# Narrower memsets between the first pass's scatters of sorted rows

## The chip, the cores and the metric

The kernel runs on one core of a Trainium2 chip. The metric is the device time of one execution in microseconds, smaller is better. Before the change it is 570.33 us, the median of three runs (570.11 to 571.1).

## The reference, cut to what matters

A block on 2 x 1024 tokens of 128 features: a mixture-of-experts layer, attention, and the same mixture again, each on a layer norm of its input.

```python
x = x + 0.5 * ffn(layernorm(x), ...)
x = x + attn(layernorm(x), ...)
x = x + 0.5 * ffn(layernorm(x), ...)

def ffn(x, sg, su, sd, rg, ru, rd, wr, rb):
    shared_out = expert(x, sg, su, sd)                  # silu(x g^T) * (x u^T), times d
    probs = softmax(x @ wr.T + rb)                      # 7 routed experts
    scores, idx = top_k(probs, 2)
    w = weights of the two, summing to 1
    out = shared_out
    for e in range(7):
        out = out + w[..., e:e + 1] * expert(x, rg[e], ru[e], rd[e])
    return out
```

## The kernel before, in words

Each token goes through the shared expert and through two of seven routed experts. Instead of computing every expert for every token, the kernel sorts: each normalised row (130 floats: 128 features, the token's number and a code for its rank) is written to DRAM (`z_rows`) at a place that belongs to its expert, twice, once for each of its two experts. Rows are then read back in tiles of 128 that belong to one expert. The first mixture layer is called the first pass here (f = 0), the one after attention the second (f = 1).

**The work of a pass.** TensorE goes through 54 jobs in a fixed order (`JOBS`): in the first pass 13 tiles of the shared expert, 38 routed tiles, and the last 3 shared tiles. A job is an up-projection (`up_pe`, L899 to L901), a multiplication with the silu on ScalarE (L1000) and VectorE (`act_dve`, L1043), three transposes (`act_tr_pe`, L919), a down-projection (`down_pe`, L933) and a copy or an addition out of PSUM (`yev_dve`, L1079 and L1081). A step of the loop in `ffn_pe` handles the up-projection of one job, the transposes of the one before and the down-projection of the one before that. Routed tiles come in batches (`BATCHES`: tiles 0-1, 2-5, 6-9, 10-11, 12-13, then fours). A batch's rows are transposed by `rows_tr_pe` (L953) when its loads have landed.

**The order of the sort.** The tokens are handled in two halves of 8 tiles. For each half VectorE computes a router (`router_dve`), the place of every row (`places_dve`, which ends with the cast to `slots`, L750), and then the lists of tiles (`segments_dve`, `lists_dve`, which ends with `rows_at`: L863 in the first half, L865 in the second). In the first 47 us VectorE also splits the routed weights in two parts: four operations of L1482, with both operands in SBUF.

GpSimd (POOL in the profile) runs `sort_part_pool` for the first and then the second half: 16 scatters each, in the order of the tiles, two for each tile. A scatter (`sort_pool`, L1174) is one indirect DMA of 128 rows. It waits for nothing of its own; the half as a whole waits for its `slots`. Behind each scatter whose tile is not the first one comes `pause_pool`: a memset (L1184) of 128 x 384 bf16 in a scratch tile, `idle`, which waits until the previous such memset is done. So the first two scatters of a pass have no memset behind them, and the other 30 have one. Nothing reads `idle`.

Behind the sort on POOL's queue come the scatters of results (`scatters_pool`, L1197), one for each routed tile, the first ten of them with the same memset, the next ones in the first pass with a memset of `keys` (L1415).

SyncE (SP) loads the sorted rows (`rows_load_sp`): it reads the tiles' places into registers (L1253), waits until all 16 scatters of the half have landed (`z_sc`), and issues one load for each tile (L1260, 65 KB). Batches 0 to 2 (tiles 0 to 9) need the first half only. Batch 3, whose first tile is tile 10, and all later ones need the second half, its lists, and 7 small DMAs of zeros that SyncE issues between the two (`pads_sp`, L1241).

The results ring has 8 buffers (`RING_Y`): VectorE's copy of routed tile n waits until the scatter of tile n - 8 has landed.

The memset in question, and what calls it:

Of the kernel before, what the change touches and what calls it, by code (L numbers as in the profile page):

```python
# [22 lines left out]
F32 = mybir.dt.float32  # L23
# [6 lines left out]
P = 128  # L30
# [33 lines left out]
HALF = TT // 2  # L64
# [219 lines left out]
def place_memory(K, ctx):  # L284
# [4 lines left out]
    def sb(name, shape, dt=F32, scope=ctx):  # L289
        return scope.enter_context(K.nc.sbuf_tensor(name, shape, dt))  # L290
# [59 lines left out]
    with ExitStack() as s:  # L350
        zt = [sb(f"zt_{part}", [P, TOKENS], F32R, scope=s) for part in ("h", "l")]
        with ExitStack() as s2:
# [8 lines left out]
            K.ys = sb("ys", [P, RING_Y, EMB], scope=s2)  # L361
            K.idle = sb("idle", [P, PAUSE], BF16, scope=s2)
            K.col_i = sb("col_i", [P, 2 * NJ + TT], mybir.dt.int32, scope=s2)
# [802 lines left out]


PAUSE = 3 * P


def sort_pool(K, f, g):

    e, (r, t) = K.nc.gpsimd, divmod(g, TT)
    e.indirect_dma_start(K.z_dram[f], bass.IndirectOffsetOnAxis(ap=K.slots[:, g:g + 1], axis=0),  # L1174
                         K.zrow[f][:, t, :], None).then_inc(K.z_sc[t // HALF], 16)
    if g % TT > 0:
        pause_pool(K, f == 1 and t < HALF)


def pause_pool(K, in_attention=False):  # L1180

    rested_pool(K)
    where = K.queries[2][:, 0:PAUSE].bitcast(F32) if in_attention else K.idle[:, :]
    K.nc.gpsimd.memset(where, 0.0).then_inc(K.rested, 1)  # L1184
    K.rests += 1


def rested_pool(K):

    if K.rests:  # L1190
        K.nc.gpsimd.wait_ge(K.rested, K.rests)
# [9 lines left out]
def sort_part_pool(K, f, h, first=0, last=SPAN):  # L1201

    e, (t0, t1) = K.nc.gpsimd, PARTS[h]
    if first == 0:
        if f == 1:
            e.wait_ge(K.blank_rows[f], 16 * FILLS * LOOPED)
        e.wait_ge(K.numbered, 2 * f + h + 1)
        e.wait_ge(K.NS[2 * f]["z"], t1 // TPC)
        e.wait_ge(K.RS["slot"], routed(f, h, "slot", 5))
    for g in [r * TT + t for t in range(t0, t1) for r in range(2)][first:last]:  # L1210
        sort_pool(K, f, g)


def scatters_pool(K, f):

    for j in range(NJ):
        if j == BATCHES[BATCH_OF[j]][0]:
            K.nc.gpsimd.wait_ge(K.FF[f]["ids"], 3 * BATCH_OF[j] + 3)
        scatter_pool(K, f, j)
        if j < WHOLE:  # L1220
            pause_pool(K)
        elif f == 0 and j < WHOLE + 2 * WIPES:
            wipe_pool(K, *divmod(j - WHOLE, WIPES))
        if f == 0 and j in FRONT_POOL:
            norm_rstd_pool(K, 1, FRONT_POOL[j])
# [1133 lines left out]
```

## Time and profile before

| | |
|---|---|
| median of 3 runs | 570.33 us |
| profiled execution | 571.84 us |
| its span, first to last instruction | 570.0 us |
| mean granted clock of TensorE | 0.972 of full |
| TensorE matmul busy | 521.1 us (91%) |
| VectorE busy | 388.5 us (68%) |
| ScalarE busy | 319.8 us (56%) |
| POOL busy | 272.1 us (48%) |

Times in the profile are microseconds from the start of the span. PE is TensorE, PEld its weight loads, DVE VectorE, ACT ScalarE, POOL GpSimd, SP SyncE. L1174 is line 1174 of the kernel. In a timeline a row has its start, its length, engine, line, operation, what it writes and reads, and in brackets how long the engine stood idle before it and what released it. The record of a scatter on POOL is the time that POOL spends on it; the data land later.

### The profile page before, as it was taken

What the parts mean: (1) busy time and instruction counts of PE and PEld (TensorE: products, weight loads), DVE (VectorE), ACT (ScalarE), POOL (GpSimd) and SP (SyncE); (2) the same over time, 40 slices, a digit from 0 to 9 for tenths busy, and PEclk for the clock granted to TensorE, in tenths of its full rate; (3) what the DMA queues carried; (4) which work ended last, traced back from release to release, by engine and by line L of the source; (5) the groups of instructions that cost most, each with busy time, mean ns of one, the idle gap of its engine ahead of it and who ended that gap; (6) DMA issues with size and microseconds to landing.
All of it is one profiled execution on the core that took longest, in us unless ns stands there. A gap on an engine that the chain in (4) does not pass through costs nothing.

```text
span 570.0 us, 11374 instructions
## 1 busy us (share of the span) xinstructions
PE 521.1 (91%) x3574; PEld 406.0 (71%) x3574; DVE 388.5 (68%) x1013; ACT 319.8 (56%) x678; POOL 272.1 (48%) x417
## 2 busy tenths in 40 slices
PE   5985969999996799999999999999999889889995
PEld 2884969998954465656666666565746889889995
DVE  5694635557367888887979888888555775445744
ACT  4552424457444276776767677677776444434643
POOL 8299887667356711212120303030318888854540
PEclk9899789999996899999999999999999999999999
DMA  8922424132861581505050505020001031431414
GB/s 283 294 67 50 111 77 120 45 107 81 242 183 56 170 190 35 173 2 175 2 174 1 176 0 176 1 102 2 2 2 33 31 91 43 118 92 34 125 50 121
DMA packets 41384, 54.65 MB, mean 96 GB/s; under 512 B 6064, under 2 KB 32176, under 8 KB 40560
## 3 DMA queue, kind: packets, MB, share of 16 engines
q1 hardware_dynamic: 32528, 42.70, 26.4%
q0 software_dynamic: 4480, 9.25, 4.9%
q10 hardware_dynamic: 4320, 1.98, 1.3%
q8 instruction: 32, 0.52, 0.4%
q14 instruction: 24, 0.20, 0.1%
HBM read 34.03 MB, written 28.00 MB: 109 GB/s over the span
## 4 chain that ended last, share of the span: by engine, by line
PE 57%; issue 18%; POOL 10%; DMA 6%; DVE 4%; SPq 2%; ACT 2%; ACTq 1%; another core or an unknown queue 1%; POOLq 0%; DVEq 0%
PE psum L1605 11%; PE psum L1648 11%; PE psum L1677 10%; PE psum L933 6%; POOL z_rows L1174 6%; PE psum L919 3%; PE psum L901 3%; PE psum L899 3%; PE psum L900 3%; PE psum L1608 2%; POOL idle L1184 2%; DMA b_p<-in_attn_c_proj_b 2%; DMA yc<-y_rows 1%; DMA y_rows<-ys,to_row 1%; PE psum L1633 1%
## 5 line engine op out<-in xcount | busy, mean ns | idle before, releaser
L1757 DVE TENSOR_REDUCE mxp<-psum 128x1 f32<-128x512 f32 (+3 forms) x304 | 179.0, 654 | 32.9 <-PE psum L1605 32.1
L1816 ACT ACTIVATE probs<-psum 128x512 f32<-128x512 f32 (+1 forms) x304 | 154.9, 578 | 39.8 <-PE psum L1648 37.2
L1863 POOL TENSOR_SCALAR_AFFINE_SELECT probs<-probs 128x512 f32<-128x512 f32 x64 | 40.0, 635 | 174.2 <-ACT probs L1816 174.2
L1648 PE MATMUL psum<-queries,keys 128*128 128x512 f32 (+3 forms) x384 | 122.5, 381 | 0.6 <-DMA queries<-m_rows 0.3
L1605 PE MATMUL psum<-keys,queries 128*128 128x512 f32 (+1 forms) x304 | 116.1, 417 | 2.9 <-DVE mxp L1757 2.4
L1000 ACT ACTIVATE silu<-psum 128x352 f32<-128x352 f32 x107 | 49.6, 463 | 99.5 <-PE psum L901 62.6
L1197 POOL DMA_INDIRECT y_rows<-ys,to_row x76 | 74.3, 977 | 59.1 <-DVE ys L1079 35.4
L1043 DVE TENSOR_TENSOR act<-silu,psum 128x352 f32<-128x352 f32 x107 | 55.6, 519 | 68.0 <-ACT silu L1000 41.7
L933 PE MATMUL psum<-wall_f,at 128*128 (+1 forms) x648 | 92.2, 279 | 2.7 <-DVE x L1081 1.8
L1648 PEld LDWEIGHTS psum<-queries,keys 128*128 128x128 f32 x384 | 66.8, 191 | 26.8 <-ACT probs L1816 12.6
L933 PEld LDWEIGHTS psum<-wall_f,at 128*128 128x128 f32 x648 | 82.1, 194 | 4.1 <-ACT at L1008 2.3
L1605 PEld LDWEIGHTS psum<-keys,queries 128*128 128x128 f32 x304 | 58.1, 194 | 18.1 <-DVE mxp L1757 7.8
L1677 PE MATMUL psum<-probs,vg 128*32 128x512 f32 (+3 forms) x768 | 69.8, 491 | 0.4 <-POOL probs L1863 0.4
L919 PE MATMUL psum<-ident,act 128*128 128x128 f32 x324 | 54.7, 278 | 5.9 <-DVE act L1043 4.4
L899 PE MATMUL psum<-wall,zs_h 128*128 x152 | 56.9, 374 | 1.0 <-issue 1.0
L1008 ACT COPY at<-psum 128x384 f32<-128x384 f32 x108 | 51.3, 475 | 11.0 <-PE psum L919 9.7
L900 PE MATMUL psum<-wall,zs_h 128*128 x152 | 50.4, 331 | 0.0
L901 PE MATMUL psum<-wall,zs_l 128*128 x152 | 50.2, 330 | 0.0
L919 PEld LDWEIGHTS psum<-ident,act 128*128 128x128 f32 x324 | 41.0, 142 | 12.3 <-DVE act L1043 8.2
L1677 PEld LDWEIGHTS psum<-probs,vg 128*32 128x32 f32 x768 | 21.1, 109 | 35.4 <-issue 22.9
L1174 POOL DMA_INDIRECT z_rows<-zrow,slots x32 | 34.4, 1076 | 15.9 <-DVE slots L750 10.5
L1174 POOL DMA_INDIRECT z_rows<-zrow_late,slots x32 | 31.2, 975 | 5.8 <-issue 5.8
(240 smaller groups left out, 732.4 us busy)
## 6 DMA issues: line engine op xcount, KB each, us to landing
z_rows<-q_stack SPq DMA_DIRECT2D x12, 682.5 KB, 5.6
keys<-k_stack SPq DMA_DIRECT2D x32, 128.0 KB, 5.9
queries<-q_stack SPq DMA_DIRECT2D x8, 512.0 KB, 5.3
zg_early<-z_rows SPq DMA_DIRECT2D x44, 65.0 KB
yc<-y_rows SPq DMA_DIRECT2D x10, 256.0 KB, 4.0
zg_late<-z_rows SPq DMA_DIRECT2D x32, 65.0 KB
k_stack<-zt_h SPq DMA_DIRECT2D x8, 256.0 KB, 2.9
q_stack<-q_h SPq DMA_DIRECT2D x8, 256.0 KB, 3.7
```

Source lines behind the costliest of these rows:

```text
L899: e.matmul(dst, zh, weight(K.wall, base, hi, HID), start=True, stop=False)
L900: e.matmul(dst, zh, weight(K.wall, base, lo, HID), start=False, stop=False)
L901: ins = e.matmul(dst, zl, weight(K.wall, base, hi, HID), start=False, stop=True)
L919: ins = e.transpose(bank(K, at_bank(f, q))[:, k * P:(k + 1) * P], K.act[:, q % 2, k * P:(k + 1) * P], K.ident[:, :])
L933: ins = e.matmul(bank(K, Y_BANK)[:, 0:EMB], K.at[:, q % 2, k * P:(k + 1) * P], weight(K.wall_f, base, DN + k * EMB, EMB), start=(k == 0), ...
L1174: e.indirect_dma_start(K.z_dram[f], bass.IndirectOffsetOnAxis(ap=K.slots[:, g:g + 1], axis=0), K.zrow[f][:, t, :], None).then_inc(K.z_sc[t ...
L1197: e.indirect_dma_start(K.y_dram[f], bass.IndirectOffsetOnAxis(ap=K.to_row[:, j:j + 1], axis=0), K.ys[:, j % RING_Y, :], None).then_inc(K.y ...
L1605: ins = e.matmul(dst, K.queries[u][:, i * P:(i + 1) * P], K.keys[u][:, heads[0]:heads[-1] + 1, k0 * P:(k0 + nb) * P], start=True, stop=Tru ...
L1648: ins = e.matmul(slot(K, u, d, n)[:, m * (q1 - q0):(m + 1) * (q1 - q0)], K.keys[v][:, j, kt * P:(kt + 1) * P], K.queries[v][:, q0:q1], sta ...
L1677: ins = e.matmul(bank(K, O_BANK)[32 * j:32 * j + 32, q0 - half * CHUNK:q1 - half * CHUNK], K.vg[:, kt, j, :], probs_of(K, n)[:, j, :], sta ...
L1757: e.tensor_reduce(K.mxp[:, heads[0]:heads[-1] + 1, i, which], scores, AX.X, ALU.max).then_inc(K.A["taken"], 1)
L1816: e.activation(probs_of(K, product)[:, heads[0]:heads[-1] + 1, :], src, ACT.Exp, scale=SCALE).then_inc(K.A["ex"], 1)
```

## The change

A memset behind a scatter of the first pass (f = 0) writes 32 columns of `idle` instead of 384. Those of the second pass, and those behind the first ten scatters of results in either pass, keep 384. The number of memsets, their order and their waits stay.

```diff
 PAUSE = 3 * P
+SHORT = P // 4
...
     if g % TT > 0:
-        pause_pool(K, f == 1 and t < HALF)
+        pause_pool(K, f == 1 and t < HALF, PAUSE if f else SHORT)


-def pause_pool(K, in_attention=False):
+def pause_pool(K, in_attention=False, columns=PAUSE):

     rested_pool(K)
-    where = K.queries[2][:, 0:PAUSE].bitcast(F32) if in_attention else K.idle[:, :]
+    where = K.queries[2][:, 0:PAUSE].bitcast(F32) if in_attention else K.idle[:, 0:columns]
     K.nc.gpsimd.memset(where, 0.0).then_inc(K.rested, 1)
```

## Rows read from the trace of the kernel before

**Rows 1.** Timeline of TensorE, the first tile behind each of two stalls

```profile
56.44 0.50 PE L953 MATMUL psum<-ident,zg_early 128*128 128x128 f32 x2 [4.90 <-DMA zg_early<-z_rows]
...
82.05 0.66 PE L953 MATMUL psum<-ident,zg_early 128*128 128x128 f32 x2 [4.67 <-DMA zg_early<-z_rows]
```

**Rows 2.** The page: busy tenths of TensorE in 40 slices of 14.25 us

```profile
PE   5985969999996799999999999999999889889995
```

**Rows 3.** The chain of waits, 76 to 82.2 us: start, length, what

```profile
76.18 2.39 DMA z_rows<-zrow,slots
...
79.76 1.88 DMA zg_early<-z_rows
```

**Rows 4.** The scatters of the first pass: duration min/median/max, first and last start

```profile
L1174 POOL DMA_INDIRECT z_rows<-zrow,slots x32: 958/964/2375, 24.8 to 76.2; - x32
```

**Rows 5.** Timeline of POOL, 24 to 53 us

```profile
26.31 0.96 POOL L1174 DMA_INDIRECT z_rows<-zrow,slots  x1 [0.30 <-issue]
27.57 0.96 POOL L1174 DMA_INDIRECT z_rows<-zrow,slots  x1 [0.30 <-issue]
...
29.13 1.52 POOL L1174 DMA_INDIRECT z_rows<-zrow,slots  x1 [0.17 <-issue]
...
32.81 0.96 POOL L1174 DMA_INDIRECT z_rows<-zrow,slots  x1 [0.16 <-issue]
...
43.48 2.38 POOL L1174 DMA_INDIRECT z_rows<-zrow,slots  x1 [0.16 <-issue]
...
51.13 0.96 POOL L1174 DMA_INDIRECT z_rows<-zrow,slots  x1 [0.17 <-issue]
52.70 0.96 POOL L1174 DMA_INDIRECT z_rows<-zrow,slots  x1 [0.16 <-issue]
```

**Rows 6.** Groups of POOL's instructions by shape: count, busy us, mean ns, idle before

```profile
L1184 POOL MEMSET idle<- 128x384 bf16 x66 | 28.7, 434 | 0.0
...
L1374 POOL MEMSET d_used<- 128x9 f32 x1 | 0.1, 97 | 0.0
```

**Rows 7.** Timeline of VectorE, 28 to 73 us

```profile
28.56 1.25 DVE L1482 TENSOR_TENSOR wall<-nat_g,wall 128x1056 fp32r<-128x1056 f32 x1
...
33.49 1.61 DVE L1482 TENSOR_TENSOR wall<-nat_g,wall 128x1408 fp32r<-128x1408 f32 x1
...
37.67 1.25 DVE L1482 TENSOR_TENSOR wall<-nat_u,wall 128x1056 fp32r<-128x1056 f32 x1
...
43.40 1.61 DVE L1482 TENSOR_TENSOR wall<-nat_u,wall 128x1408 fp32r<-128x1408 f32 x1
...
46.85 0.54 DVE L750 CAST slots<-d_slot 128x16 int32<-128x16 f32 x1
...
72.77 0.25 DVE L865 SCALAR_TENSOR_TENSOR rows_at<-d_raw,d_start,tile 128x28 int32<-128x28 f32 x1
```

**Rows 8.** Register loads of the tiles' places on SyncE: min/median/max ns

```profile
L1253 SPq TENSOR_LOAD <-rows_at x22: 463/872/1068, 35.7 to 503.8; - x22
```

**Rows 9.** Stretches: length, busy time by engine, granted clock, DMA share, GB/s

```profile
77.00:80.50 3.50, 0.39 (x4) 0.19 (x2) 0.71 (x2) 0.37 (x2) 3.17 (x6) 1.00 0.19 57
80.50:82.00 1.50, 0.00 (x0) 0.00 (x0) 0.00 (x0) 0.00 (x0) 1.33 (x3) 0.51 0.43 107
486.44:488.31 1.87, 0.00 (x1) 0.03 (x1) 0.33 (x2) 0.00 (x0) 1.55 (x3) 1.00 0.49 141
```

**Rows 10.** Timeline of TensorE: up-projections behind the second stall

```profile
82.37 0.64 PE L899 MATMUL psum<-wall,zs_h 128*128 x1
...
88.82 0.41 PE L899 MATMUL psum<-wall,zs_h 128*128 x1
...
93.19 0.41 PE L899 MATMUL psum<-wall,zs_h 128*128 x1
```

**Rows 11.** DMA queues, 24 to 29 us: packets, MB, share of 16 engines

```profile
q0 software_dynamic: 4, 0.01, 1.3%
```

## The prediction

> **What bounds the kernel now.** I read the waits of TensorE first, then its timeline around the longest ones, then the chain of waits back from there, and last the timelines of the engines that the chain names. Between 40 and 90 us TensorE stands still twice for gathered rows [rows 1]. The first gathered tile is transposed at 56.44 after 4.90 us without work, so the shared tiles ahead of it end at 51.54; the eleventh tile, the first of the second half's list, comes at 82.05 after 4.67, so TensorE was free at 77.38. From 85.5 to 171 us every slice of the page has TensorE busy nine tenths or more [rows 2], so what the second stall gives up moves everything behind it.
>
> The chain behind the second stall [rows 3]: the last scatter starts at 76.18 and lands 2.39 later, SyncE issues the loads, the load takes 1.88, and TensorE starts at 82.05. That is 5.87 us from the start of the 32nd scatter. The first stall has the same form: the 16th scatter starts at 51.13 [rows 5], and TensorE follows 5.31 us later. POOL works through the 32 scatters in one piece, from 24.8 to 76.2 with a median of 964 ns each [rows 4], and is on the chain all that time.
>
> **What a pause costs.** Two scatters with no memset between them start 1.26 us apart (26.31, 27.57); with one, 1.57 (51.13, 52.70) [rows 5]: 0.96 for the scatter, 0.43 for the memset, 0.17 until the next. A memset of 384 columns takes 434 ns and one of 9 columns 97 [rows 6], 0.90 ns a column, so I put one of 32 columns at 0.12 (estimate from the two). Then 0.96 + 0.12 + 0.17 = 1.25, no less than the 1.26 that scatters take without a memset, and I take 1.26. Each pause gives 0.305. The lower end is nothing at all, if a scatter grows by what the pause loses (a rival below); the upper is 0.315.
>
> **First half.** 13 pauses stand ahead of the 16th scatter; 13 x 0.305 would be 4.0. But scatters are also held up by VectorE. L1482 runs four times with two operands in SBUF [rows 7], and a scatter that starts inside one is long: that of 29.13 ends at 30.65, 0.84 after the op's end at 29.81; that of 43.48 (2.38 long) ends at 45.86, 0.85 after 45.01 [rows 5, 7]; the two others repeat the pattern. As an undisturbed scatter lasts 0.96, it seems to need what VectorE holds (the port, below) some 0.12 after its start. With that I walk the new order, VectorE's times left as they are. The 4th starts at 28.83 inside the first op and ends at 30.65 as before. The 7th starts at 33.47, needs the port at 33.59, inside the op of 33.49, and ends at 35.94 as before. The 9th starts at 37.50, needs it at 37.62, just before the op of 37.67, and goes through; the 10th (38.76) ends at 39.76. The 14th starts at 43.84 inside the last op and ends at 45.85, so the 15th starts at 46.15 and the 16th at **47.41 instead of 51.13: 3.7 us**. If the 9th is caught after all (0.05 decides), the 16th starts at 48.67: 2.5. If the 7th escapes too, 5.0. I take 3.7.
>
> The second half's scatters wait for their places (the cast L750, done at 47.39 [rows 7]). The 17th would start at 48.67, so it does not wait. Of POOL's queue nothing else stands between.
>
> **Second half.** 16 steps from the 16th to the 32nd, 0.305 each: 4.9 us. Two lists ops of VectorE in that stretch also have two operands in SBUF and could hold a scatter for up to 0.5 each; they are short beside a step of 1.26, so I take off 0.2 (ends 0 and 1.0). The last scatter then starts at 76.18 - 3.7 - 4.9 + 0.2 = 67.8 and its rows reach TensorE at 67.8 + 5.87 = 73.7: **8.4 us** earlier.
>
> **Is TensorE there by then, and what is late next?** It starts the routed tiles at 47.41 + 5.31 = 52.7 and had 20.8 us of work from there to the second stall; part of that ran at half clock after the first stall, which now is 1.2 us. Without it TensorE is ready at about 71.1 and waits 2.6 us. The places of the second half's tiles (L865) are ready at 73.02 today [rows 7], 16.6 after the first gathered tile. They follow TensorE's steps, so they come at 52.7 + 16.6 - 2.4 = 66.9; with SyncE's register load, 0.87 [rows 8], 67.8. The landing of the last scatter, 67.8 + 2.39 = 70.2, is still the later one. The scatters of results that are queued behind on POOL start 8.4 us earlier as well and keep their own 384-column pauses; their first is needed when its ring slot comes round, eight tiles later, so they cost nothing.
>
> **The clock of TensorE.** After the 4.67 us stall the granted clock was 1.00 until 80.5, 3.1 us after the last matmul, then 0.51; a stall of 1.87 us in the second pass kept 1.00 [rows 9]. At 1.2 GHz, from the first up-projection at 82.37 to the third at 88.82, the work took 6.45 us; the next two tiles at 2.4 GHz, with a larger batch to transpose, took 4.37 (88.82 to 93.19) [rows 10]. Allowing 0.3 for the first transposes and the smaller batch, the low clock costs 2.4. The new second stall of 2.6 lies between the two cases. Gain: 2.4 if the clock stays, 0 if it falls as before, -0.7 if it falls just as TensorE resumes (1.5 us more of work at the low clock, at 2.4 per 5.25). The nearer row is the one that falls, so I take 1.0.
>
> **Sum:** 3.7 + 4.9 - 0.2 + 1.0 = 9.4 us. Against the profiled execution's 571.84 (span 570.0 and 1.84 around it, which the change does not touch) that gives 562.4; the runs shown have a median of 570.33, 1.5 less, so the forecast is 561.0 us.
>
> **Rivals.**
> *The lists become the bound* (0.14). Denser scatters hold up VectorE's small casts: L750 took 0.54 for 16 columns [rows 7]. Five such ops stand in the lists of the second half; if each waits one scatter more (0.96), they end 4.8 later, 2.4 past the last landing's margin of 2.4 (70.2 - 67.8). The gain falls to 7.0, or 6.0 if the clock falls: 563 to 564.5. Against: VectorE came in between POOL's ops so far.
>
> *The op that starts first holds the port* (0.07). Then the 9th scatter, started 0.17 before L1482, would delay that op to 38.46; it would end at 39.71, the 10th scatter at 40.55 instead of 39.76, and the gain is 0.8 less: 561.8. The trace speaks against it: a scatter started at 32.81 [rows 5] and L1482 still began inside it at 33.49 and took its usual 1.61 [rows 7]. The Trainium skill (SBUF — State Buffer, SBUF: two separate sides) has this rule: whichever of the two starts first has the shared pair for the whole instruction and the other blocks fully. By that rule the time is 561.8; the trace agrees that a scatter inside L1482 is blocked, not that L1482 is blocked by a scatter.
>
> *The queue of scatters fills: slower* (0.08). POOL starts scatters faster than they land. If only two may be on their way, a step is at least half a landing: 1.2 us at 2.39, no harm; it is slower than today's 1.57 from a landing of 3.13 on. The place is the first 30 us, where loads fill the DMA engines: of the first three scatters only 4 packets had moved by 29.0 [rows 11], so the first took over 4.2 to land. If that held throughout, a step is 2.1, the last scatter starts at 24.8 + 31 x 2.1 = 89.9 and the kernel ends 13.7 later, at 584. Against: the fourth scatter started with three on their way.
>
> *The change does not shorten the step* (0.07): the scatter grows by what the memset loses, since nothing shows more than three scatters without a pause. Then 570.3.
>
> **How the numbers follow.** The forecast has 0.64. Its own range: best 5.0 + 4.9 + 2.4 = 12.3, 558.0; worst 2.5 + 4.9 - 1.0 - 0.7 = 5.7, 564.6. All terms at one end together are unlikely, so 558.8 to 564. With the lists' case the range reaches to 564.8, and holds these two, the port's case at 561.8, less the tails: some 0.8. A measurement tells 0.2%, 1.1 us, from no change. Faster: 0.64 + 0.14 + 0.07 = 0.85; same 0.07; slower 0.08.
>
> **What would show it.** Memsets of about 0.12 and scatter starts 1.26 apart in the second half; 16th scatter at 47.4 (48.7 if the 9th is caught), 32nd near 67.8; TensorE's first stall about 1.2 with the clock kept, its second 2.6. Scatters longer than 0.97 outside VectorE's L1482 and lists ops would prove me wrong; so would a load of the second half that is issued more than 2.5 us after the last scatter's start (lists), or an unmoved 82.05.

## The result and the profile after

The change makes the kernel slower: 581.74 us at the median of five executions (579.7 to 585.89) against 571.1 for the kernel before on the same chip (570.11 to 574.8), a ratio of 1.0171 with a 95% interval of 1.0133 to 1.0209. The forecast was 561.0. The profiled execution took 585.89, with a span of 584.2; it lies 4.15 above the median, so what is read from it is a little too large.

POOL does what was forecast. In its timeline (start, length, engine, line, operation, and in brackets the idle time before it and its releaser; every line number behind 1168 is one higher than before) the short memset takes 0.14 to 0.15 us and the scatters start 1.27 apart, where [rows 5] had 1.57:

```profile
44.67 0.96 POOL L1175 DMA_INDIRECT z_rows<-zrow,slots  x1 [0.17 <-issue]
45.62 0.15 POOL L1185 MEMSET idle<- 128x32 bf16 x1
45.94 0.96 POOL L1175 DMA_INDIRECT z_rows<-zrow,slots  x1 [0.17 <-issue]
46.89 0.15 POOL L1185 MEMSET idle<- 128x32 bf16 x1
60.78 0.96 POOL L1175 DMA_INDIRECT z_rows<-zrow,slots  x1 [13.74 <-DVE slots L750]
```

By shape, 30 of the memsets are short, and the scatters' median is that of [rows 4] (count: min/median/max in ns, first and last start):

```profile
L1175 POOL DMA_INDIRECT z_rows<-zrow,slots x32: 958/964/1673, 25.2 to 79.8; - x32
...
L1185 POOL MEMSET idle<- x66: 138/432/443, 29.0 to 515.5; 128x384 bf16 x36, 128x32 bf16 x30
```

The 16th scatter starts at 45.94, not 51.13. But then POOL stands still for 13.74 us: the places of the second half, written by VectorE's L750, come at 59.80, not at 46.85 [rows 7]. So the question is why VectorE is 13 us late. Its timeline has four waits that ended with "remote" (the releaser is none of the work that the view can match in time):

```profile
34.71 0.29 DVE L1081 SCALAR_TENSOR_TENSOR x<-psum,x 128x128 f32<-128x128 f32 x1 [1.63 <-remote]
...
40.44 0.29 DVE L1081 SCALAR_TENSOR_TENSOR x<-psum,x 128x128 f32<-128x128 f32 x1 [2.56 <-remote]
...
48.31 0.29 DVE L1081 SCALAR_TENSOR_TENSOR x<-psum,x 128x128 f32<-128x128 f32 x1 [3.26 <-remote]
...
59.80 0.17 DVE L750 CAST slots<-d_slot 128x16 int32<-128x16 f32 x1
...
83.44 0.29 DVE L1081 SCALAR_TENSOR_TENSOR x<-psum,x 128x128 f32<-128x128 f32 x1 [8.86 <-remote]
```

L1081 adds the down-projection of TensorE (L933) to x. In TensorE's timeline that down-projection was over long before:

```profile
69.00 1.49 PE L933 MATMUL psum<-wall_f,at 128*128 128x128 f32 x6
...
77.69 0.87 PE L919 MATMUL psum<-ident,act 128*128 128x128 f32 x3 [4.99 <-issue]
83.88 1.62 PE L933 MATMUL psum<-wall_f,at 128*128 128x128 f32 x6 [5.32 <-DVE x L1081]
```

It ended at 70.49, VectorE started at 83.44, and TensorE itself then waited for VectorE. ScalarE, which also reads what TensorE writes, shows the same in its timeline:

```profile
73.56 0.46 ACT L1000 ACTIVATE silu<-psum 128x352 f32<-128x352 f32 x1 [6.72 <-PE psum L901]
77.11 0.48 ACT L1008 COPY at<-psum 128x384 f32<-128x384 f32 x1 [3.08 <-issue]
83.50 0.58 ACT L1017 CAST zs_h<-psum 128x512 fp32r<-128x512 f32 x1 [5.91 <-remote]
```

The trace also holds the times at which semaphores were updated. For the last matmul of a down-projection (L933), its recorded end and the update of its semaphore in the changed kernel:

```
end of L933      32.74  36.05  42.05 | 50.37  52.95  56.10  58.52 | 62.21  64.17  70.49 | 85.49
its update       34.69  40.41  48.29 | 50.39  52.96  56.11  58.53 | 62.22  65.02  83.42 | 85.51
late by           1.95   4.36   6.24 |  0.02   0.01   0.01   0.01 |  0.01   0.85  12.93 |  0.02
scatters on POOL ----- 25 to 47 ---- | ------- none ------------- | ----- 61 to 81 ---- | none
```

The updates come in order. They are late only in the two trains of scatters, by more the longer a train has run (the one at 62.22, near the start of the second, is on time), and they are on time in the gap between the trains. In the changed kernel 19 of the 48 updates by TensorE that are recorded from 26 to 92 us came more than 0.1 us after the last matmul that could have made them; of VectorE's 73, ScalarE's 25 and POOL's 5 none did, and before the change none of TensorE's 49. ("Late" below is counted this way, which is a lower bound; the trace doesn't have every update. For POOL it is thin: of the updates by its 30 memsets in the two trains the trace has 5, where it has all 32 of the kernel before from 24 to 82 us.)

In the chain of waits back from 106 us, the four waits of VectorE stand as time that no recorded work explains, 16.2 us together:

```profile
33.08 1.61 another core or an unknown queue
...
37.88 2.53 another core or an unknown queue
...
45.05 3.24 another core or an unknown queue
...
74.58 8.84 another core or an unknown queue
```

The stretch from 24 to 48 us, one row for the kernel before and one after (length, busy time of PE, PEld, DVE, ACT, POOL with counts, granted clock, DMA share, GB/s), shows three engines with less done in the same time, and DMA engines far from full:

```profile
24.00:48.00 24.00, 20.90 (x155) 19.40 (x153) 20.09 (x63) 12.88 (x23) 20.82 (x24) 1.00 0.35 85
```

```profile
24.00:48.00 24.00, 16.43 (x108) 14.55 (x106) 10.02 (x32) 8.80 (x15) 19.05 (x30) 0.86 0.41 100
```

VectorE's products (L1043) serve as milestones. The 15th of them and the 23rd, which lies behind both trains, before:

```profile
64.67 0.52 DVE L1043 TENSOR_TENSOR act<-silu,psum 128x352 f32<-128x352 f32 x1 [0.41 <-issue]
...
88.38 0.52 DVE L1043 TENSOR_TENSOR act<-silu,psum 128x352 f32<-128x352 f32 x1 [1.20 <-PE psum L919]
```

and after:

```profile
85.44 0.51 DVE L1043 TENSOR_TENSOR act<-silu,psum 128x352 f32<-128x352 f32 x1
...
103.50 0.52 DVE L1043 TENSOR_TENSOR act<-silu,psum 128x352 f32<-128x352 f32 x1 [0.71 <-issue]
```

The 15th is 20.8 us late, the 23rd 15.1, and the span 14.1 longer (584.2 against 570.0). So in this execution the whole loss is made in the first 104 us. The page's line of TensorE shows the place: in [rows 2] the third to the sixth of the 40 slices read 8, 5, 9 and 6 tenths, now 7, 6, 6 and 3 (a slice is 14.6 us).

```profile
PE   6876639999997779999999999999999889899995
```

### The profile page after: what moved, and what is told of

Same layout as the page of the kernel before. It is cut to its first block, busy times and chain, and to the rows that moved or that the text cites. A ratio compares the mean times of both kernels' runs of the same rounds, so it can differ in the third digit from the quotient of the medians.

```text
span 584.2 us, 11374 instructions
## 1 busy us (share of the span) xinstructions
PE 524.0 (90%) x3574; PEld 407.7 (70%) x3574; DVE 388.2 (66%) x1013; ACT 319.5 (55%) x678; POOL 261.9 (45%) x417
## 4 chain that ended last, share of the span: by engine, by line
PE 62%; issue 18%; DVE 6%; DMA 6%; another core or an unknown queue 3%; POOL 2%; SPq 2%; ACT 1%; ACTq 1%; DVEq 0%; POOLq 0%
PE psum L1606 11%; PE psum L1649 11%; PE psum L1678 9%; PE psum L933 8%; PE psum L919 4%; PE psum L899 4%; PE psum L900 4%; PE psum L901 4%; PE psum L1609 2%; DMA b_p<-in_attn_c_proj_b 2%; DMA yc<-y_rows 2%; DMA y_rows<-ys,to_row 1%; PE psum L1634 1%; DVE wall L1483 1%
## 5 line engine op out<-in xcount | busy, mean ns | idle before, releaser
L1043 DVE TENSOR_TENSOR act<-silu,psum 128x352 f32<-128x352 f32 x107 | 55.5, 519 | 74.6 <-ACT silu L1000 38.3
L933 PE MATMUL psum<-wall_f,at 128*128 (+1 forms) x648 | 93.9, 282 | 10.9 <-DVE x L1081 8.9
L933 PEld LDWEIGHTS psum<-wall_f,at 128*128 128x128 f32 x648 | 83.4, 197 | 13.1 <-issue 10.4
L1649 PEld LDWEIGHTS psum<-queries,keys 128*128 128x128 f32 x384 | 66.8, 191 | 26.8 <-ACT probs L1817 12.6
L899 PE MATMUL psum<-wall,zs_h 128*128 x152 | 56.2, 370 | 3.2 <-issue 3.0
L919 PEld LDWEIGHTS psum<-ident,act 128*128 128x128 f32 x324 | 41.0, 142 | 20.4 <-DVE act L1043 10.6
L900 PE MATMUL psum<-wall,zs_h 128*128 x152 | 49.9, 328 | 0.0
L1175 POOL DMA_INDIRECT z_rows<-zrow,slots x32 | 32.5, 1017 | 29.6 <-DVE slots L750 24.4
```

What stands on the lines that cost most here:

```text
L899: e.matmul(dst, zh, weight(K.wall, base, hi, HID), start=True, stop=False)
L900: e.matmul(dst, zh, weight(K.wall, base, lo, HID), start=False, stop=False)
L919: ins = e.transpose(bank(K, at_bank(f, q))[:, k * P:(k + 1) * P], K.act[:, q % 2, k * P:(k + 1) * P], K.ident[:, :])
L933: ins = e.matmul(bank(K, Y_BANK)[:, 0:EMB], K.at[:, q % 2, k * P:(k + 1) * P], weight(K.wall_f, base, DN + k * EMB, EMB), start=(k == 0), ...
L1649: ins = e.matmul(slot(K, u, d, n)[:, m * (q1 - q0):(m + 1) * (q1 - q0)], K.keys[v][:, j, kt * P:(kt + 1) * P], K.queries[v][:, q0:q1], sta ...
```

## The experiments

The theory after the result (A): while scatters follow each other closely, TensorE's semaphore updates are delivered late, as in a queue that empties when the scatters leave room. Each ratio below is to the kernel before on the same chip, with its 95% interval. Times in us are medians; lateness and all times inside a run come from its one profiled execution.

**Which half.** 32 columns in the first half's train alone, then in the second half's alone.

```diff
-        pause_pool(K, f == 1 and t < HALF, PAUSE if f else SHORT)
+        pause_pool(K, f == 1 and t < HALF, SHORT if f == 0 and t < HALF else PAUSE)
```

> Theory A (spacing): when scatters start 1.27 us apart, TensorE's semaphore updates are delivered late, in a queue that empties when the train ends; 1.57 us apart it stays empty. Then the first half behaves as in the changed kernel (VectorE's slots, L750, near 59.8 us; the 17th scatter near 60.8) and the second half starts its scatters 1.57 apart, so the 32nd is near 84.3; TensorE's updates are prompt from 61 us on; time 577 to 585. Theory B (only the second train hurts, the wait for the slots being an accident of it): the 17th scatter near 48 to 50 and 566 to 569.

Measured: 571.34 us, ratio 1.000 (0.9963 to 1.0037). Neither forecast held. TensorE's updates were at most 0.4 us late up to 38 us and then up to 5.9, so the slots came at 50.81 instead of the 59.8 that A expected; the 17th scatter still waited for them 6.20 us and started at 51.80. What the shorter train earned was given back by that wait. Why the same train delayed updates only from 38 us on here, and from 31 us on in the changed kernel, is open.

```diff
-        pause_pool(K, f == 1 and t < HALF, PAUSE if f else SHORT)
+        pause_pool(K, f == 1 and t < HALF, SHORT if f == 0 and t >= HALF else PAUSE)
```

> Theory A (spacing): the first half as before the change (16th scatter 51.1, slots 46.9); the second train's scatters start 1.27 apart, the 32nd near 71.8, and TensorE's updates are late between 53 and 74 us, by up to 10 us, so VectorE and ScalarE stand idle there; the rows arrive earlier but the work ahead of them is late; time 570 to 576. Theory B, that the loss is the first half's alone (the wait for the slots): the second train brings its 4.4 us and the time is 565 to 567.

Measured: 578.19 us, ratio 1.011 (1.0042 to 1.0178). The first half is as before the change (slots 46.41), the 32nd scatter starts at 71.30, and TensorE's updates are up to 11.65 us late, until 75.0. Counted from the first scatter the last one is 4.4 us earlier, and still the kernel is slower, by 2 us more than A forecast: theory A, not B.

**Spacing, or the width of the memset.** Three short memsets in a row in place of one wide one.

```diff
-        pause_pool(K, f == 1 and t < HALF, PAUSE if f else SHORT)
+        for _ in range(1 if f else 3):
+            pause_pool(K, f == 1 and t < HALF, PAUSE if f else SHORT)
```

> Three memsets of 32 columns, one behind the other, in place of one of 384: the same columns an instruction as in the change, but scatters start about 1.6 to 1.7 us apart. Theory A (spacing): no late updates of TensorE, slots near 47 to 48, 571 to 576 (the last scatter 0 to 4 us later than before). Theory C (the wide memset itself is needed, whatever the spacing; its rows of writes keep something free): late updates as in the changed kernel, and 580 or more.

POOL's timeline, a scatter, its three memsets (one row) and the next scatter:

```profile
61.06 0.96 POOL L1175 DMA_INDIRECT z_rows<-zrow,slots  x1 [0.16 <-issue]
62.02 0.50 POOL L1186 MEMSET idle<- 128x32 bf16 x3
62.68 0.96 POOL L1175 DMA_INDIRECT z_rows<-zrow,slots  x1 [0.16 <-issue]
```

1.62 us apart. Measured: 574.51 us, ratio 1.0036 (1.0005 to 1.0067); three updates late, by 1.0 at most, where A had said none. Most of the changed kernel's loss, and its updates up to 12.9 us late, are gone with memsets just as narrow, so the width of a memset is not what decides: theory A, and C falls. (But scatters 1.62 apart delay three updates here, and 1.57 apart, with one wide memset, none.)

**No memset at all.**

```diff
-    if g % TT > 0:
+    if g % TT > 0 and f == 1:
```

> No memset between the first pass's scatters at all: 1.26 us apart, POOL has neither the short memsets nor their waits and updates. Theory A (spacing): as the changed kernel, updates of TensorE late by 6 us and more, 578 to 586. Theory E (it is the many short memsets with their semaphores, not the density of scatters, that hold TensorE's updates up): no late updates, the 16th scatter near 46 and 560 to 565.

Measured: 578.25 us, ratio 1.0121 (1.0084 to 1.0158), starts 1.27 apart, updates up to 10.5 us late. Short memsets with their semaphores are not the cause either: E falls.

**The dose.** Only the constant changes: 128, 256, 288, 320 and 352 columns.

```diff
-SHORT = P // 4
+SHORT = 5 * P // 2
```

> 128 columns in place of 32: scatters start about 1.34 us apart. Theory A with a queue that empties at a rate set by the room between scatters: late updates still, but fewer; slots between 48 and 59 us; 571 to 580. Theory A with a sharp edge between 1.27 and 1.57: either as the changed kernel (580 to 586) or, with prompt updates, 563 to 567.

> 256 columns: scatter starts 1.46 us apart (1.27 at 32 columns, 1.35 at 128, both with late updates of TensorE; 1.57 at 384, none). Theory A, a queue of TensorE's updates that empties only as fast as the room between scatters allows: late updates still, smaller than the 12.6 us of 128 columns, and no gain: 569 to 575. Theory A with a sharp edge below 1.46: no late updates, 32nd scatter 3 us earlier than at 384, 566 to 568.

> 288 columns: scatter starts 1.485 us apart, between 256 (1.46, updates up to 4.6 us late, no gain) and 320 (1.51, up to 1.8 late, 0.75% faster). Theory A (room between scatters lets a certain number of TensorE's updates through): lateness between the two, 1.8 to 4.6 us, and 567 to 571. A rival, that 320 was faster by chance of the chip: 570 to 572 here and at 320 again.

> 320 columns: scatter starts 1.51 us apart. Theory A, gradual: a few updates up to 2 us late, time 568 to 572, no change that can be told. Theory A with an edge below 1.51: none late, the 32nd scatter 1.5 us earlier, 568 to 569.5. If the loss came from the shorter memset itself rather than from the spacing, this kernel would lose about 1.7 us (one sixth of the change's 10.6).

> 320 columns once more, beside 288 and 352. If the gain is real: 565.5 to 569 and a ratio of 0.990 to 0.996; if it was chance: 570 to 572.

> 352 columns: scatter starts 1.54 apart. Theory A: updates at most 1 us late, the trains 0.8 us shorter than with 384; 568 to 570.5, so that the best width lies at 320 or near it.

All of them by columns (the first pass; "lists" is the time from the first scatter to VectorE's L865, the places of the second half's tiles; "profiled" is the time in us of the execution that these two are read from, "median" that of all; medians come from several chips and compare by the ratio):

```
columns      starts apart   latest update   lists   profiled   median   ratio (95%)
none         1.27           10.5            60.9    578.96     578.25   1.0121 (1.0084 to 1.0158)
32 (change)  1.27           12.9            70.0    585.89     581.74   1.0171 (1.0133 to 1.0209)
128          1.35           12.6            57.1    571.96     575.64   1.0057 (1.0026 to 1.0088)
256          1.46            4.6            54.5    572.67     571.07   0.9982 (0.9956 to 1.0009)
288          1.48            4.5            54.4    570.42     571.64   0.9986 (0.9955 to 1.0018)
320          1.51            1.8            48.5    567.7      567.15   0.9925 (0.9896 to 0.9954)
320 again    1.51            3.2            48.7    571.16     570.04   0.9952 (0.9926 to 0.9977)
352          1.54            0.9            46.3    570.12     570.2    0.9954 (0.9928 to 0.9979)
384 (before) 1.57            0.0            48.0    571.84     571.1    1
```

Lateness shrinks with the room between scatters, and the median time follows it, both by and large only. The first three rows are not in the order of their spacings, the largest drop in lateness is between 1.35 and 1.46, and the execution with 128 columns that was read took 571.96 us with an update 12.6 us late. No edge separates kernels without harm from the others. (320 did better than the gradual case forecast, 288 a little worse.) At 256 the last scatter starts 3.7 us earlier, counted from the first scatter, but the lists come 6.5 later, and nothing is gained. With 320 and 352 columns the kernel is **faster than both**: by 0.5 to 0.75% in three measurements on two chips (the intervals reach from 0.2 to 1.0%). The rival that 320 was chance falls with its second measurement, by the ratio: its 570.04 us lies in the range that was put down for chance, but the kernel before took 573.0 on that chip, and 0.9952 lies in the range put down for a gain. Which of the two widths is the better one can't be told.

At 320 columns the first time, the timeline of TensorE has the two places of [rows 1] as follows, the first and the last row. Both are still waits for rows, of 3.21 and 0.66 us instead of 4.90 and 4.67; between them stands a wait of 0.82 for VectorE:

```profile
55.37 0.41 PE L953 MATMUL psum<-ident,zg_early 128*128 128x128 f32 x2 [3.21 <-DMA zg_early<-z_rows]
...
76.24 0.93 PE L933 MATMUL psum<-wall_f,at 128*128 x6 [0.82 <-DVE ys L1079]
...
79.80 0.41 PE L953 MATMUL psum<-ident,zg_early 128*128 128x128 f32 x2 [0.66 <-DMA zg_early<-z_rows]
```

and the stretch around the last row, first in the kernel before, then with 320 columns, shows what the short stall brings: the granted clock stays at 1.00, where it was 0.66 after a stall of 4.67.

```profile
80.00:90.00 10.00, 7.95 (x42) 7.87 (x43) 3.01 (x11) 2.52 (x6) 8.23 (x13) 0.66 0.45 119
```

```profile
80.00:90.00 10.00, 9.26 (x69) 8.66 (x68) 5.14 (x18) 4.08 (x10) 8.63 (x13) 1.00 0.49 130
```

**The same mean spacing, unevenly.** Three short pauses, then three memsets of 384 in a row.

```diff
-        pause_pool(K, f == 1 and t < HALF, PAUSE if f else SHORT)
+        long = f == 0 and g >= TT and t % 2
+        for _ in range(3 if long else 1):
+            pause_pool(K, f == 1 and t < HALF, PAUSE if f or long else SHORT)
```

> Three pauses of 32 columns, then three memsets of 384 in a row: scatters 1.27 apart in groups of four, with 2.6 us behind each group; the mean spacing is 1.6, as before the change. Theory A (a queue that fills while scatters are dense and empties in a gap): updates late by 1 to 4 us inside a group, never more, as each gap empties it; slots (L750) 0 to 4 us later than before; 570 to 576. Theory D (each dense pair does its own lasting harm, in proportion to the number of dense pairs, three quarters of the change's): 578 to 582.

```profile
34.84 0.97 POOL L1175 DMA_INDIRECT z_rows<-zrow,slots  x1 [0.16 <-issue]
35.81 0.14 POOL L1187 MEMSET idle<- 128x32 bf16 x1
36.11 0.97 POOL L1175 DMA_INDIRECT z_rows<-zrow,slots  x1 [0.16 <-issue]
37.07 1.40 POOL L1187 MEMSET idle<- 128x384 bf16 x3
38.63 0.97 POOL L1175 DMA_INDIRECT z_rows<-zrow,slots  x1 [0.16 <-issue]
```

Measured: 570.91 us, ratio 0.9989 (0.9961 to 1.0018). Updates are up to 2.9 us late and do not pile up. Two overdue ones arrive at 38.0, in the middle of the three memsets of 37.07: POOL's memsets let them through, and in a gap the backlog goes. Theory A, not D.

**Another place.** 384 columns in the first pass, 32 in the second (in its first half these memsets write `queries`, so that the width had to be passed on there too).

```diff
-        pause_pool(K, f == 1 and t < HALF, PAUSE if f else SHORT)
+        pause_pool(K, f == 1 and t < HALF, SHORT if f else PAUSE)
...
-    where = K.queries[2][:, 0:PAUSE].bitcast(F32) if in_attention else K.idle[:, 0:columns]
+    where = K.queries[2][:, 0:columns].bitcast(F32) if in_attention else K.idle[:, 0:columns]
```

> 384 columns in the first pass as before the change, 32 in the second pass. Theory A holds for any stretch in which TensorE's updates are waited for: scatters 1.27 apart between 429 and 480 us, updates late by several us there, VectorE and ScalarE idle, and 573 to 582. Rival: the hold-up needs something of the first pass (its loads from DRAM, its shared tiles, cold code); then nothing is late in the second pass and the last scatter comes up to 9 us earlier, 562 to 568.

Measured: 592.35 us, ratio 1.0324 (1.0273 to 1.0374), more than A forecast; updates up to 14.5 us late. Its waits from 430 to 495 us (who waited for whom: total, times, longest):

```profile
ACT silu L1000 <- issue: 14.0, 2, 13.7
DVE act L1043 <- issue: 11.3, 2, 9.2
...
POOL z_rows L1175 <- DVE slots L750: 9.8, 1, 9.8
```

Nothing of the first pass is needed for it.

**What about a scatter does it.** Both kernels start from the last one. In the first, each scatter of the second pass carries 8 bytes a row, not 520 (it leaves out the 128 features): the target is the same DRAM seen as rows of two words, and L750 computes 65 times the place plus 64.

```diff
+    src, dst = K.zrow[f][:, t, :], K.z_dram[f]
+    if f:
+        src, dst = src[:, ID:ROW], dst.rearrange("r (a c) -> (r a) c", c=2)
-    e.indirect_dma_start(K.z_dram[f], bass.IndirectOffsetOnAxis(ap=K.slots[:, g:g + 1], axis=0),
-                         K.zrow[f][:, t, :], None).then_inc(K.z_sc[t // HALF], 16)
+    e.indirect_dma_start(dst, bass.IndirectOffsetOnAxis(ap=K.slots[:, g:g + 1], axis=0),
+                         src, None).then_inc(K.z_sc[t // HALF], 16)
```

> As with 32 columns in the second pass alone (592.4), but each of that pass's scatters carries only the 8 bytes of a row's number and code, not its 520: the sorted tokens of the second pass are left out (zeros stand in their place). If the bytes that the scatters move hold TensorE's updates up (theory F), nothing is late and the time is 562 to 572. If it is the scatters themselves, 128 indexed rows each, whatever a row holds (theory G): updates late by 5 us and more between 430 and 495, and 586 to 596.

Measured: 593.05 us, ratio 1.0377 (1.0309 to 1.0444), updates up to 13.1 us late. POOL's timeline is that of full rows, 0.96 us a scatter and 1.27 apart:

```profile
467.52 0.96 POOL L1182 DMA_INDIRECT z_rows<-zrow_late,slots  x1 [8.62 <-DVE slots L753]
468.48 0.14 POOL L1192 MEMSET idle<- 128x32 bf16 x1
468.79 0.96 POOL L1182 DMA_INDIRECT z_rows<-zrow_late,slots  x1 [0.17 <-issue]
```

The bytes do not matter: F falls. In the second kernel each scatter of 128 rows is two of 64, the places of the upper 64 partitions copied to a tile of their own.

```diff
+    if f:
+        for k, index in enumerate((K.slots[0:P // 2, g:g + 1], K.slots_low[:, g:g + 1])):
+            if k:
+                pause_pool(K, t < HALF, SHORT)
+            e.indirect_dma_start(K.z_dram[f], bass.IndirectOffsetOnAxis(ap=index, axis=0),
+                                 K.zrow[f][k * P // 2:(k + 1) * P // 2, t, :], None).then_inc(K.z_sc[t // HALF], 16)
...
```

> As with 32 columns in the second pass alone, but each scatter of 128 rows there is two of 64, with a pause of 32 columns behind each; the rows are all written. Two of them should take 1.4 to 1.9 us if a scatter of 64 rows takes 0.45 to 0.65, and 2.5 if POOL's time does not depend on the rows. If the rate of indexed rows decides (theory G1) and 128 rows take 1.55 or more: no update later than 2 us, 568 to 576. If the number of scatters decides, each holding the updates up (theory G2), with one every 0.7 to 0.95 us: late as in that kernel or worse, 590 to 610. If a pair takes 2.5: nothing late, and slower by the longer trains alone, 580 to 600.

```profile
468.19 0.90 POOL L1184 DMA_INDIRECT z_rows<-zrow_late,slots  x1 [0.17 <-issue]
469.09 0.14 POOL L1197 MEMSET queries<- 128x32 f32 x1
469.40 0.90 POOL L1184 DMA_INDIRECT z_rows<-zrow_late,slots_low  x1 [0.17 <-issue]
```

Half the rows cost POOL 0.90 us, not half of 0.96, so this is the case of a pair that takes 2.4, for which I had put down that nothing would be late. Measured: 640.13 us, ratio 1.1177 (1.1125 to 1.123), and updates up to 19.2 us late; the time also holds the trains that are twice as long. Rows a microsecond (64 in 1.21, 53) are fewer here than before the change (128 in 1.57, 82), and so are the bytes. So neither decides. What is left is how closely scatters follow each other (1.21 apart), or POOL's share of time in them (0.90 of 1.21, 74%; 76% in the changed kernel, 64% at 320 columns, 61% before). These two could not be parted, since POOL's time for a scatter hardly depends on its rows; nor is either parted from the semaphore increments of the landings, 16 for each scatter (`then_inc` in the diff above). That G2 said "late or worse" for a spacing below 0.95 and the lateness came at 1.21 is a miss in the size of POOL's step.

In this kernel POOL's own updates are late too. A memset waits for the update of the one before it; for the memset that ended at 523.06 that update came at 525.73, 2.66 us later, and for the next one 2.61 later (POOL's timeline):

```profile
525.77 0.12 POOL L1197 MEMSET idle<- 128x32 bf16 x1 [1.66 <-remote]
...
528.56 0.12 POOL L1197 MEMSET idle<- 128x32 bf16 x1 [1.60 <-remote]
```

So the delay is not TensorE's alone; of VectorE's and ScalarE's recorded updates in that stretch (425 to 560 us) none is late.

## Why the prediction was wrong

The forecast was a gain of 9.4 us and the median shows a loss of 10.6. By its own steps:

- **The step of a scatter: right.** 0.305 us less was forecast, 0.30 is measured (1.57 to 1.27); the memset takes 0.14 to 0.15, not 0.12. Behind the first one no scatter outside VectorE's L1483 lasts over 0.97, and the rivals of a queue that fills and of a step that does not shorten fall.
- **The first half: too small, and outside its own ends.** From the first scatter to the 16th the train takes 20.71 us in place of 26.36, 5.65 less; I had taken 3.7, between 2.5 and 5.0. Two scatters, not three, ran into VectorE's L1482 (now L1483), and lasted 1.67 us each. VectorE was so late that the other two of these operations came behind the train, at 50.62 and 56.34.
- **"With that I walk the new order, VectorE's times left as they are": the step that failed.** In it lay the assumption that the other engines keep their pace when POOL's scatters come closer. VectorE's times moved by 13 us, because TensorE's signals to it were up to 6.2 us late in that train. From it followed the next sentence, "The 17th would start at 48.67, so it does not wait": it waited 13.74.
- **The second half: fifteen of the sixteen steps of 0.3 were there (60.78 to 79.82, 1.27 each; the first was the wait), on a start 8.1 us later than before**, and with updates up to 12.9 us late, so that TensorE's own work ahead of the gathered rows was late as well.
- **TensorE's readiness.** Forecast 71.1 (the 20.8 us of work in that sum are 20.94 by [rows 1]; it changes little). In fact TensorE stood still for 4.99 us up to 77.69 and 5.32 up to 83.88, waiting for VectorE and ScalarE. The two stalls for gathered rows, which were to shrink to 1.2 and 2.6, are gone, because TensorE comes to the rows later than the rows do: at 64.01 to the first tile (forecast 52.7), at 99.65 to the eleventh (forecast 73.7), and neither row of its timeline has a wait.

```profile
64.01 0.38 PE L953 MATMUL psum<-ident,zg_early 128*128 128x128 f32 x2
...
99.65 0.38 PE L953 MATMUL psum<-ident,zg_early 128*128 128x128 f32 x2
```

- **The lists as the bound.** That rival named the right engine, VectorE, but as a matter of small casts held up by scatters, 4.8 us in all. No small cast was held up (L750 took 0.17 us, not 0.54); the lists came 22 us later than before, counted from the first scatter, as they stand behind VectorE's waits. The sign that the prediction named for this rival did appear: SyncE issues the first load of the second half at 96.23, 16.4 us after the last scatter's start, not within 2.5.
- **The slower rival** had scatters queueing behind each other, with 584 us, near the 581.74 that came, but by another way: no scatter waited for another, and in the second train all sixteen start 1.27 apart.
- **The clock: right where it could be seen.** At 320 columns the second stall for rows is 0.66 us and the clock around it stays at 1.00. From the eleventh tile's transposes to the 23rd product of VectorE it takes 4.12 us there (79.80 to 83.92) and 6.33 in the kernel before (82.05 to 88.38). The difference, 2.2, is close to the 2.4 that the prediction put on the low clock. A stall of 2.6, on which its choice of 1.0 rested, occurred in neither.

**Could it have been seen before?** Partly. The chain of waits of the kernel before, from 490 to 510 us, where scatters of results start 1.56 apart, has these rows:

```profile
497.96 1.02 another core or an unknown queue
...
499.62 0.94 another core or an unknown queue
...
501.07 0.98 another core or an unknown queue
```

There TensorE's updates are up to 2.2 us late already, and three rows with no known releaser say so. The prediction did not read that stretch. How steeply it gets worse below 1.5 no row of that trace shows. Nor is the spacing all of it: the second pass's scatters of sorted rows, as close to each other up to 484 us, delay no update by more than 0.15. What is different from 494 on was not tried (the DMA engines are busy for 49% of the time from 494 to 503 and for 23% from 447 to 484).

**Shown and open.** Shown: TensorE's updates are late when scatters start closely, by and large the later the less room there is (seven spacings from 1.27 to 1.57 in the first pass, 1.21 and 1.27 in the second); the memset's width, its semaphores, the bytes and the rows of a scatter do not decide. Open: by which path a scatter on POOL holds up TensorE's updates, and POOL's own in one kernel, but none recorded of VectorE and ScalarE; and whether the recording of updates, which loses many of POOL's in the same stretches, has a part in it. The Trainium skill (Perfetto Trace Analysis, Per-instruction lifecycle: what the profiler-reported window actually captures) says that the end of a matmul in a profile is estimated and that its semaphore update follows only when the write of the result is acknowledged. The trace agrees that the two are separate events: 0.01 to 0.02 us apart in the gap between the trains, 12.93 inside one. Whether the acknowledgement or the update's delivery is slow, it can't tell; no run here tells it either. The Trainium skill (VectorE: DVE Perf Modes, The TRN2 errata — SBUF-src ops pay a fixed extra latency per instruction) warns that semaphore increments at a high rate from one engine can deadlock another, and advises to space dense ones. Delays were seen here, no deadlock. Taking out the memsets' increments did not help; whether those of the landings are the reason was not tried.

## What to carry to other kernels

An instruction that seems to do nothing between two DMAs that POOL issues may be the room in which another engine's signals get through; before shortening such a pause, look in the trace for waits whose releaser had long been done ("remote", "unknown queue") and whether they stand where POOL issues scatters closely. When a pause is a dose, try several: here 32 columns lose 1.7%, and 320 and 352 gain 0.5 to 0.75%. And a walk of a new order must move the other engines too; a check that costs little is to ask, for each time that is "left as it is", which signals it depends on.

## What was not expected of the hardware

TensorE's semaphore updates can come 12.9 us (in one kernel 19.2) after the recorded end of the matmul, while VectorE's and ScalarE's, as far as they are recorded in the stretches read, come within 0.1 us; POOL's too, but for the kernel of 64-row scatters, where some came up to 2.7 late. A scatter of 64 rows takes POOL 0.90 us and one of 128 rows 0.96, and one of 8 bytes a row as long as one of 520. Scatters 1.27 us apart are enough to delay TensorE's by 12.9, with the DMA engines busy for 41% of the time in the stretch shown above.
